# Mamba scan on one core: GpSimd instead of VectorE builds the diagonals of B for batches 1 to 7, between its products

## The reference

```python
hs_res = hidden_states @ w_in.T
hs, res = (hs_res[..., :d_in], hs_res[..., d_in:])        # d_in = 512
hs = silu(causal_conv(hs, w_conv))                        # 4 taps
x_dbl = hs @ w_xproj.T
dt, Bm, Cm = x_dbl[..., :64], x_dbl[..., 64:80], x_dbl[..., 80:]
delta = softplus(dt @ w_dt.T + b_dt)
# for each of 512 channels d and 16 states n:
#   z[t] = exp(delta[t, d] * A[d, n]) * z[t-1] + delta[t, d] * hs[t, d] * Bm[t, n]
#   y[t, d] = sum over n of z[t] * Cm[t, n], plus hs[t, d] * D[d]
y = y * silu(res)
return y @ w_out.T
```

## Time and profile before

| | |
|---|---|
| median of 3 runs | 3835.36 us (3832.68 to 3845.11) |
| profiled execution | 3848.53 us, its span 3846.7 us |
| Mamba phase in the trace | about 60 to 1795 us: 8 batches of some 218 us |
| one `make_diag` on DVE | 2.28 us (median of 32) |
| one product on POOL | 2.376 us (median of 512) |
| one scan on DVE | 2.281 us (median of 512) |
| granted TensorE clock, mean over the span | 0.964 of full speed |

### The profile page before, as it was taken

The page is one execution under the profiler, slowest core; times in us unless marked ns, Lnnn a source line. Parts: engine busy times, 40 slices in busy tenths (PEclk is TensorE's granted clock), DMA queues, the critical chain, the costliest instruction groups (busy, mean ns, idle before and its releaser), DMA issues.

```text
span 3846.7 us, 121218 instructions
## 1 busy us (share of the span) xinstructions
PE 3570.1 (93%) x52170; PEld 1610.9 (42%) x52170; DVE 3331.1 (87%) x3617; ACT 2611.6 (68%) x3895; POOL 1724.5 (45%) x1054
## 2 busy tenths in 40 slices
PE   5999999999999999997499999999999999999997
PEld 3555555554545555554232323324233242332422
DVE  5899899989889999985899797897978979789796
ACT  4665657666665757663169496694976949769498
POOL 4787878878787878875410200202002020020200
PEclk8999999999999999999799999999999999999999
DMA  3544445444444535442430603306034060230600
GB/s 94 136 125 109 139 107 136 121 128 112 131 116 106 155 98 138 123 123 63 101 42 2 110 2 60 52 2 99 13 44 68 2 99 13 44 68 2 90 11 13
DMA packets 145113, 307.59 MB, mean 80 GB/s; under 512 B 24456, under 2 KB 64016, under 8 KB 144336
## 3 DMA queue, kind: packets, MB, share of 16 engines
q1 hardware_dynamic: 144592, 299.94, 34.5%
HBM read 230.66 MB, written 35.13 MB: 69 GB/s over the span
## 4 chain that ended last, share of the span: by engine, by line
PE 23%; ACT 11%; issue 10%; DVE 7%; POOL 0%; DMA 0%; ACTq 0%; SPq 0%; DVEq 0%; POOLq 0%
ACT probs L1500 9%; PE ps L1310 6%; PE ps L1297 5%; PE ps L1416 5%; DVE neg_max L1625 3%; PE ps L1345 2%; PE ps L1258 2%; PE ps L1325 1%; PE ps L1358 1%; ACT o_sb L1507 1%; PE ps L1442 1%; DVE acc L1761 1%; ACT m_rows L1513 1%; DVE diag_b L1783 1%; DVE x1T L1591 1%
## 5 line engine op out<-in xcount | busy, mean ns | idle before, releaser
L350 POOL TENSOR_TENSOR z<-z,c_rep 128x1024 f32<-128x1024 f32 x512 | 1413.3, 2771 | 337.7 <-DVE z L867 329.3
L1500 ACT ACTIVATE probs<-ps,e_scale 128x512 f32<-128x512 f32 x2048 | 1242.9, 690 | 132.1 <-PE ps L1297 117.2
L867 DVE TENSOR_TENSOR_SCAN z<-dA,ps 128x1024 f32<-128x1024 f32 x512 | 1158.1, 2279 | 137.3 <-PE ps L408 89.7
L1625 DVE TENSOR_REDUCE neg_max<-ps 128x1 f32<-128x1024 f32 x1024 | 1204.4, 1219 | 46.7 <-PE ps L1258 42.0
L708 ACT ACTIVATE dA<-rep,a_rep 128x1024 f32<-128x1024 f32 x512 | 566.3, 1144 | 218.3 <-DVE z L867 215.0
L1297 PE MATMUL ps<-q_st,k_st 50*128 50x512 f16 x2048 | 676.9, 393 | 29.8 <-ACT probs L1500 17.7
L408 PEld LDWEIGHTS ps<-diag,u_t 64*64 64x64 f32 x32768 | 532.1, 135 | 393.9 <-issue 393.7
L1310 PE MATMUL ps<-probs,v_h 128*32 128x256 f32 x8192 | 658.1, 396 | 0.6 <-ACT o_sb L1507 0.6
L408 PE MATMUL ps<-diag,u_t 64*64 64x64 f32 x32768 | 599.7, 222 | 62.5 <-DVE z L867 40.0
L1244 POOL COPY v_h<-v_all 128x80 f32 (+1 forms) x256 | 62.6, 246 | 1282.5 <-PE ps L1310 1282.5
L1258 PE MATMUL ps<-k_st,q_st 48*128 48x512 f16 x2048 | 582.8, 393 | 3.7 <-DVE neg_max L1625 3.5
(11 more groups left out here) (189 smaller groups left out, 3089.0 us busy)
## 6 DMA issues: line engine op xcount, KB each, us to landing
c_rep<-c_scratch SPq DMA_DIRECT2D x512, 256.0 KB, 4.0
rep<-delta SPq DMA_DIRECT2D x128, 256.0 KB, 4.5
q_st<-qk_halves SPq DMA_DIRECT2D x192, 128.0 KB, 9.8
k_st<-qk_halves SPq DMA_DIRECT2D x192, 128.0 KB, 10.5
qk_halves<-qk_parts SPq DMA_DIRECT2D x32, 512.0 KB, 10.7
x_nat<-in_x SPq DMA_DIRECT2D x9, 1024.0 KB, 8.4
x_rows<-x_nat SPq DMA_DIRECT2D x9, 1024.0 KB, 7.0
xT<-in_xT SPq DMA_DIRECT2D x8, 1024.0 KB, 7.7
```

The lines of the kernel that those rows point to most:

```text
L350: pool.tensor_tensor(z[:, k % ZR, :], z[:, k % ZR, :], c_rep[:, slot, :], ALU.mult).then_inc(s_zc, 1)
L867: dve.tensor_tensor_scan(z[:, k % ZR, :], dA[:, k % AR, :], pair(1 + k % 2), 0.0, ALU.mult, ALU.add).then_inc(s_z, 1)
L1500: act.activation(probs[:, kt, half * HALF:(half + 1) * HALF], ps[:, ring_bank(("probs", h, 2 * kt + half)), :], ACT.Exp, scale=e_scale[:, ...
L1625: dve.tensor_reduce(neg_max[:, qt:qt + 1], pair(qt % 2), AX.X, ALU.max, negate=True).then_inc(s_mx, 1)
```

## The change

`make_diag` is written a second time, in POOL's block, and POOL issues it for every batch but the first: part 3 after the product of unit 7, parts 0, 1 and 2 of the next batch after the products of units 60, 61 and 63. DVE keeps `make_diag` for batch 0 only. The waits of `dbx` on `s_dg` and the arithmetic stay.

```diff
@@ block.gpsimd
-            def units(b):
+            def make_diag(c, part):
+
+                pool.wait_ge(s_bc, c + 1)
+                first, last = part * 4, (part + 1) * 4
+                turned = b_t[:, :].rearrange("p (i n) -> p i n", n=NS)
+                pool.tensor_tensor(diag[:, :, first:last, :],
+                                   eye[:, :].unsqueeze(1).unsqueeze(1).broadcast_to([P, NI, 4, TB]),
+                                   turned[:, :, first:last].unsqueeze(3).broadcast_to([P, NI, 4, TB]), ALU.mult).then_inc(s_dg, 1)
+
+            def units(b, more):
                 for k in range(U):
...
                     pool.tensor_tensor(z[:, k % ZR, :], z[:, k % ZR, :], c_rep[:, slot, :], ALU.mult).then_inc(s_zc, 1)
+                    if k == 7 and b:
+                        make_diag(b, 3)
+                    if k == 60 and more:
+                        make_diag(b + 1, 0)
+                    if k == 61 and more:
+                        make_diag(b + 1, 1)
+                    if k == 63 and more:
+                        make_diag(b + 1, 2)
...
@@ block.vector
-                    if k == 9 and b:
-                        make_diag(b, 3)
...
-                    if k == 59 and more:
-                        make_diag(c, 0)
-                    if k == 60 and more:
-                        make_diag(c, 1)
...
-                    if k == 63 and more:
-                        make_diag(c, 2)
```

More of the change, by code:

```diff
@@ L350, in units @@
                     pool.tensor_tensor(z[:, k % ZR, :], z[:, k % ZR, :], c_rep[:, slot, :], ALU.mult).then_inc(s_zc, 1)
+                    if k == 7 and b:
[6 more added lines that the diff above has]
+                        make_diag(b + 1, 2)
             first_conv()
             for b in range(NB):
-                units(b)
+                units(b, b < NB - 1)
         @block.tensor
```

## The result

The changed kernel takes 3877.43 us (median of 4 runs, 3874.55 to 3879.48) against 3838.16 us for the kernel before in the same comparison (4 runs, 3832.68 to 3845.11). The ratio is 1.0101, with a 95% interval from 1.0081 to 1.0121: 39 us slower, 31 to 46. The forecast was slower by 56 us; 3877.43 lies in the range of 3858 to 3908.

The account below looks back on a forecast made before the run. PE was taken as the bound, waiting for `make_u` at seven borders. 7 x 8.0 = 56 us on the profiled 3848.53 gave 3904.5, and 13.2 less for the median 3891.5, say 3892 us (+1.5%); range 3858 to 3908.

Parts of the forecast that it names:

- the rival with `make_u` first: At the border `make_u` gets the port before part 1: 4.7 us lost per border, 3868 us; chance 0.15.
- What bounds the kernel: PE bounds the Mamba phase almost everywhere; DVE time counts only where PE waits, 4.4 us for `make_u` at each border.
- What DVE gains: The 28 instructions leaving DVE, 64 us, are worth at most 0.8 us at each of seven borders, 5.5 us.
- What a part costs on POOL: One part as a POOL instruction: 4.4 us taken, from 3.8 below to 4.75 above, up to 5.3 in the range.
- Steps 1 to 6: At the border `log_error` waits for part 0, `make_delta` for product 61, `make_u` for part 1; `make_u` ends 6.3 us later.
- Step 7: After `make_u`, late products make `log_error` at unit 4 wait, another 1.6 us; together 7.9, say 8.0 us per border.
- A second term: After PE's longer idle at the border, PE may be slow for about 1 us longer; included in the range.
- Part 3 costs nothing: Part 3 on POOL after product 7 is in time, with no two-input DVE instruction near: no loss.
- only late products: Parts let DVE in between, only POOL's lateness counts: 1 to 2 us per border, 3842 to 3849 us; chance 0.07.
- not slower: DVE's two-input steps hardly wait for parts, products stay in time: 7 x 0.8 us won, 3830 us; chance 0.05.
- a much dearer part: A part takes 6 us or more on POOL, each further us costing 2 per border: 3910 and more; chance 0.02.

Follow-up runs that it names:

- the ceiling run: Against the kernel before, no engine builds the diagonals for batches 1 to 7: 3828.35 against 3838.44 us, ratio 0.9977.
- the merged parts: As the change, but parts 1 and 2 are one GpSimd instruction of 4096 elements after product 61: 3894.54 against 3841.11 us for the kernel before, ratio 1.0158.
- its own run: Against the kernel before, only part 3 is built on POOL, parts 0 to 2 stay on DVE: 3839.29 against 3839.54 us, ratio 0.9998.
- the memsets: As the change, but POOL writes each part with two memsets that read nothing: 3842.81 against 3841.11 us for the kernel before, ratio 1.0009.
- the version with the parts out of the way: As the change, but DVE builds part 0 at k = 59 and part 1 at k = 63: 3839.55 against 3841.11 us for the kernel before.
- the halves: As the change, but every part on POOL is two instructions of 1024 elements: 3859.62 against 3841.11 us for the kernel before, ratio 1.0047.
- part 1 in the gap: As the change, but part 0 on DVE at k = 59, POOL's part 1 waits for `make_u`: 3834.50 against 3838.44 us for the kernel before.
- part 0 on DVE: As the change, but part 0 is back on DVE at k = 59: 3851.13 against 3839.54 us for the kernel before, ratio 1.0034.

## Why the prediction was right, and where its sizes were off

The direction, the place and the order of the waits were right. The size was not: 39 us were lost where 56 were forecast, and the result owes its place in the stated range to the width of that range. 3877.43 lies just below what the forecast gave itself (3878 to 3908); the stated range reached down to 3858 only because it took in the rival with `make_u` first, which did not happen. The step that was mis-sized is the cost of a part on POOL. By the prediction's own numbers, 8.0 us per border with 4.4 us and 6.2 with 3.8, a part of 3.63 gives an estimate of 5.7 per border, 40 us in all.

- **What bounds the kernel.** Right. PE's wait for `make_u` grew from 4.4 to 10.2 us per border (near 11 was said), PE's waits for scans did not grow (35.0 us against 40.0), and removing all the parts gains 10 us (4 to 14), not 64.
- **What DVE gains, at most 5.5 us.** Too low by half, by the traces: the ceiling run gives 10 us with an interval that still holds 5.5, but `make_u` can end 1.46 us earlier, not 0.8: with part 1 gone from DVE, product 61 is over when Ln is done, and `make_delta` takes 1.2 instead of 1.93. I had counted only its earlier start.
- **What a part costs on POOL.** Here the prediction missed: 4.4 was taken, 3.8 was called the lower bound, and it is 3.63. The bound was twice the 1895 ns of a product with a broadcast operand, and doubling one instruction counts what is spent once per instruction twice. Halves of 1024 elements take 1.90 us in the row further down, two of them 3.80, a whole 3.63. Neither the scans beside it nor the three steps of its pattern made it dearer than that row.
- **Steps 1 to 6.** Right in order and mechanism, each of them visible in the rows above. `log_error` 4.19 (some 5 was said), `make_delta` 1.92 (2), `make_u` 4.52 (5.4). `make_u` ends 4.7 us later, not 6.3. The part enters twice, and twice the 0.77 us that it is shorter is 1.5 of the 1.6.
- **Step 7.** The `log_error` at k = 4 waits 1.2 us more than before in the median, 1.6 was said. A second term did not appear: I let PE be slow for about 1 us longer behind a longer idle stretch. The transposes take 1.97 us in both kernels, and the adds behind them took 3.68 us at this border before, behind 4.42 us of idle, and take 3.01 now, behind 10.16. These adds vary from border to border, from 2.4 to 3.7 us before and from 2.6 to 3.4 with the change. From `make_u`'s end to `dbx` of unit 0 it is 5.2 us before, 4.8 with the change and 5.1 with the merged parts (means over the seven), where PE idles for 13.4 us: no growth with the idle stretch. A border loses 4.9 us at `dbx` of unit 9 (means over the seven), 34 in all, against 39 measured (31 to 46) and 56 forecast; the 5 us between are within the interval and stay open.
- **Part 3 costs nothing.** Right, by its own run.
- **The rivals.** `make_u` keeping the port, only late products, not slower and a much dearer part are all out by the timeline, the length of a part and the memsets. Of the late products a piece is true, in another form: lateness makes DVE meet products in flight at k = 4 and 5. That took the gain of the version with the parts out of the way.
- **The page's rule.** By the Trainium skill's page "SBUF — State Buffer", section "Who interferes with whom", the one that issues first has the port for its whole instruction, and a GpSimd instruction that only writes does not contend. The trace agrees in both: 7.95 us of `make_u` behind an instruction of 8.03, and no wait of `log_error` or `make_u` for the 56 memsets. Who gets in when both wait is another matter; the last section has what the runs show of it.

## What to carry to other kernels

A two-input instruction on SBUF that goes to GpSimd is not off VectorE's path because another engine runs it. Here VectorE's own instructions with two SBUF inputs stood still for as long as it lasted, up to 6.7 us for one of 4096 elements, while scans and `relu_less_error`, with one, did not. Look at what the two engines issue at the same moment on the critical chain, not at their busy shares. Before work is moved, a run without that work at all tells what the move can win; here it was some 10 us in all, against 6.3 us of new waits of `log_error` and `make_u` at each of seven borders.

## What the runs showed of the hardware that was not expected

**A waiting VectorE instruction is sometimes passed over.** In the twelve traces together, `log_error`, `make_delta` or `make_u` waited some 250 times for a GpSimd instruction behind which another one was queued, and got in before that one (the next one's row starts within 0.1 us of the first one's end and is the longer by the VectorE instruction). Twice it did not. In the kernel with the halves, at one border of seven (POOL's timeline):

```profile
519.99 2.35 POOL L360 TENSOR_TENSOR z<-z,c_rep 128x1024 f32<-128x1024 f32 x1
...
522.30 2.34 POOL L360 TENSOR_TENSOR z<-z,c_rep 128x1024 f32<-128x1024 f32 x1
```

And DVE's, with a half of a part from POOL for its duration:

```profile
520.53 5.20 DVE L825 SCALAR_TENSOR_TENSOR sp_e<-sp_w,sp_e 128x1024 f32<-128x1024 f32 x1
```
```profile
511.13 1.90 POOL L349 TENSOR_TENSOR diag<-eye,b_t 128x1024 f32<-128x1024 f32 x1
```

`log_error` came up 0.54 us into one product and let that and the next one by, ending 1.1 us after the second. With part 1 in the gap, a `log_error` at k = 4 of one border (4.29 us) did the same. In both cases no product was queued behind the second. Why is open; no run tries it. Apart from these, nine instructions came up within 0.05 us of the end of a GpSimd instruction, `make_delta` at all seven borders with part 0 on DVE among them, and there the queued GpSimd instruction went first each time.

**Where the scatter of the runs comes from, in part.** The kernel before varies by 12 us over the four runs of the first comparison, and by up to 22 us over the 23 of a later one. In its profile, inside batch 1, PE stands still for 2.03 us in the middle of one unit's `dbx`, with no releaser, and the four products behind it take 3.49 us instead of 1.94 (timeline of PE; it lists each of these products twice, so that the 32 products of a `dbx` are x64 and the four of an `add` x8):

```profile
395.01 0.91 PE L408 MATMUL ps<-diag,u_t 64*64 64x64 f32 x42
397.94 0.66 PE L408 MATMUL ps<-diag,u_t 64*64 64x64 f32 x22 [2.03 <-issue]
398.53 3.49 PE L427 MATMUL ps<-z,eye 128*64 128x512 f32 x8
```

Over that stretch the granted clock is 0.95 of full speed, over one of the same work in the next batch 1.00 (busy time by stretch; the clock is the third number from the end):

```profile
380.00:414.00 34.00, 30.91 (x716) 16.47 (x716) 25.91 (x14) 25.34 (x32) 25.59 (x11) 0.95 0.51 150
602.00:631.00 29.00, 28.33 (x719) 15.67 (x714) 25.32 (x13) 24.18 (x31) 24.48 (x10) 1.00 0.58 166
```

At 1.0 the clock is 2.4 GHz, and 3.49 us for what takes 1.94 elsewhere is near what its lower level of 1.2 GHz would give (3.88). What held PE up in those 2.03 us the profile does not say. The changed kernel's profile has such a stop too, a longer one:

```profile
1075.65 1.08 PE L425 MATMUL ps<-diag,u_t 64*64 64x64 f32 x30 [4.87 <-issue]
```

From one border to the next the kernel before has two batches of 221.5 and 222.0 us, with stops of 2.03 and 2.95 us in them, where three others have 216.6 to 216.8; the changed kernel has one of 228.4, with the stop of 4.87, where four others have 221.1 to 221.8. So the batches with the longer stops take some 5 to 7 us more, in either kernel; a stop of 1.58 us in another batch of the kernel before (219.4 us) cannot be judged so, as that batch is longer than its neighbours in the other kernels, too. The stops do not explain why the two profiled executions differ by only 26 us where the medians differ by 39: some 10 us in one trace and 7 in the other nearly cancel. Part of it is which executions were profiled, 3848.53 us for a kernel with a median of 3838.16, and 3874.55 us, the shortest of four, for the other.
